# Layer 1 attention: VectorE does `finish` between the maxima and the row sums of a batch

## The chip, the core and the metric

The kernel runs on one core of a Trainium2 chip. The metric is the device time of one execution in microseconds (us). The engines are PE (TensorE, matrix products), DVE (VectorE), ACT (ScalarE), POOL (GpSimd) and SP (SyncE, which issues the DMAs here). Each engine runs its own list of instructions in order; engines wait for one another with semaphores that count up.

## What is computed

A four layer decoder with gated cross attention: x is 1024 x 128, the context 6404 x 128. Each layer adds an attention over the context and a feed forward block. The change lies in the attention of layer 1 alone:

```
mu = jnp.mean(x, axis=-1, keepdims=True)
var = jnp.mean(jnp.square(x - mu), axis=-1, keepdims=True)
xn = (x - mu) * jax.lax.rsqrt(var + EPS) * ln_g + ln_b
q = _split_heads(xn @ Wq)                    # 16 heads of 64
kv = xn @ Wkv
k = _split_heads(kv[..., :INNER])
v = _split_heads(kv[..., INNER:])
mem = _split_heads(memories @ Wm)
k = jnp.concatenate([k, mem], axis=2)        # 1024 + 6404 = 7428 keys
v = jnp.concatenate([v, mem], axis=2)
dots = jnp.einsum('bhid,bhjd->bhij', q, k) * scale
attn = jax.nn.softmax(dots, axis=-1)
out = jnp.einsum('bhij,bhjd->bhid', attn, v)
...
return out @ Wo + bo
```

## The kernel before

`l1_attention` works in 32 units. A unit is one head and one half (512) of the queries. The 7428 keys are 59 tiles of 128 (the last one of 4), and four tiles are a batch, so that a unit has 15 batches, 0 to 14.

In a batch PE does, in this order: two scorings for maxima (`max_score`, L893, bf16, each 128 queries against 1024 keys; they belong to a unit ahead), the exact scores of the four tiles (L915 and L916), an extra if the batch has one, and the weighing of the values of the batch before (L927). ACT turns each score tile into `prob` with Exp (L1031). The row sums of `prob` are shared out: DVE adds the first two tiles of a batch into `tot_d` (`total_up`, L1082; the unit's first tile is a copy, L1079), POOL the other two into `tot_p` (L1134). DVE also takes the maxima of the scorings out of PSUM (`maximum`, L1059), and the units' negated maximum (L1068) goes back through PE into the scores of the next unit.

An extra stands in a batch as `extra_of(u, b)` says. Batch 1 of every unit but the first has "fin": `finish(u - 1)`, in which PE multiplies the weighed values with Wo (L942) and sums the row sums over the partitions (L944), and DVE takes the reciprocal (L1092) and adds the result to y (L1095, four instructions). The other extras prepare the next pair of heads. With u mod 4 = 0 or 1, batches from 4 on (9 and 8 of them) have a "k": a K or Q projection on PE (L869), rounded by ACT (`round_hi`, L985), whose rest DVE takes (`cut_lo`, L1051). With u mod 4 = 3, batches 2 to 14 have a "v": a V projection (L882), copied out by ACT; with u mod 4 = 0 batches 0 and 2 have one too. The last four units have no "k", and no "v" from batch 2 on of unit 31.

Scorings for maxima and extras share two pairs of PSUM banks in turn. Whoever takes a pair waits for the one that had it two places earlier:

```
def take_slot(n):
    if n >= 2:
        by_dve, by_act = freed[n - 2]
        if by_act:
            pe.wait_ge(v_out, by_act)
        if by_dve:
            pe.wait_ge(released, by_dve)
    return slot(n)
```

So in a batch with an extra the order of the places is: first maximum scoring, second maximum scoring, extra. The extra waits for DVE's first maximum of its own batch, and the second maximum scoring of the next batch waits for the extra to be emptied: by `finish` (L1095) or `cut_lo` (L1051) on DVE, or by ACT. Within DVE's list, a batch is: two maxima, two row sums, the extra.

Of the kernel before, what the change touches and what calls it, by code (L numbers as in the profile page):

```python
# [588 lines left out]
def l1_attention(c, w, scratch):  # L589
# [32 lines left out]
    def f32(ap):  # L622
        return ap.bitcast(FP32)

    def rows_of(t):
        return min(P, KEYS - t * P)
# [4 lines left out]
    def extra_of(u, b):  # L631
        p, i = divmod(u, 4)
        if b == FIN_AT:
            return ("fin", u - 1) if u >= 1 else None
        if i == 0 and p >= 1 and b in (0, 2):
            return "v", (p, BATCHES - 2 + b // 2)
        if p + 1 == PAIRS:
            return None
        if i < 2 and 4 <= b <= 12 and 9 * i + b - 4 < JOBS:
            return "k", (p + 1) * JOBS + 9 * i + b - 4  # L640
        if i == 3 and b >= 2:
            return "v", (p + 1, b - 2)
        return None

    def max_steps(u, b):
        first = STEPS * (u + 1) + LEAD + PER_BATCH * b
        return [divmod(n, STEPS) for n in range(first, first + PER_BATCH) if n < STEPS * UNITS]
# [23 lines left out]
    def slot(n):  # L671
        return 4 + 2 * (n % 2)

    def ring_no(u, t):
        return 1 + (TILES + 1) * u + t + (1 if t >= BATCH * (NM_AT + 1) and u + 1 < UNITS else 0)

    def nm_no(u):
        return 0 if u == 0 else 1 + (TILES + 1) * (u - 1) + BATCH * (NM_AT + 1)

    def step_at(i):  # L680
        if i < UQ * FULL:
            return [(i // FULL, (i % FULL) * CH, CH)] * 2
        return [(2 * (i - UQ * FULL) + half, FULL * CH, REM) for half in range(2)]

    def dve_tiles(b):
        return [t for t in tiles_of(b) if t % BATCH < 2]
# [16 lines left out]
    with ExitStack() as held:  # L703
# [17 lines left out]
        with phase(nc, "loaded") as (block, loaded):  # L721
            @block.sync
            def _(sp):
                sp.dma_start(gain[:], w["ln_g"].partition_broadcast(P)).then_inc(loaded, 16)
                sp.dma_start(shift[:], w["ln_b"].partition_broadcast(P)).then_inc(loaded, 16)
                sp.dma_start(bo[:], w["bo"].partition_broadcast(P)).then_inc(loaded, 16)
                for base in (0, DH):
                    sp.dma_start(Wo_twice[0][base:base + DH, :], w["Wo"][0:DH, :]).then_inc(loaded, 16)
                sp.wait_ge(loaded, 16 * 9)
# [19 lines left out]
        with phase(nc, "chain", "scored", "exped", "weighed", "slotted", "released", "v_out", "hi_out", "cast_out",  # L749
# [104 lines left out]
            def _(pe):  # L854
# [9 lines left out]
                def project(k):  # L864
                    p, (kind, src, a, n, _) = k // JOBS, jobs[k % JOBS]
                    bank = take_slot(slot_no["k", k])
                    if p >= 1:
                        pe.wait_ge(weights_in[p % 2], 64 * ((p + 1) // 2))
                    nc.tensor.matmul(c.banks(bank)[:, 0:n], weights[p % 2][:, kind, :], src[:, a:a + n],  # L869
                                     start=True, stop=True).then_inc(slotted, 1)  # L870
# [173 lines left out]
            @block.vector  # L1044
            def _(dve):
                link = Chain(dve, chain)

                def cut_lo(k):
                    n, m = slot_no["k", k], jobs[k % JOBS][3]
                    dve.wait_ge(hi_out, k + 1)  # L1050
                    nc.vector.tensor_tensor(lo_s[k % DEPTH][:, 0:m], c.banks(slot(n))[:, 0:m],  # L1051
                                            f32(hi_s[k % DEPTH][:, 0:m]), ALU.subtract).then_inc(released, 1)

                def maximum(u, i):
                    n = slot_no["max", (u, i)]
                    dve.wait_ge(slotted, n + 1)
                    j, _, _ = step_at(i)[0]
                    if i < UQ * FULL:
                        nc.vector.tensor_reduce(mx[:, u % 2, j, i % FULL:i % FULL + 1], c.banks(slot(n), 2), AX.X,  # L1059
                                                ALU.max).then_inc(released, 1)  # L1060
                    else:
                        nc.vector.tensor_reduce(mx[:, u % 2, j:j + 2, FULL], c.ps[:, slot(n):slot(n) + 2, 0:REM], AX.X,
                                                ALU.max).then_inc(released, 1)
                    if i == STEPS - 1:
                        dve.wait_ge(released, freed[n][0])
                        if u >= 2:
                            dve.wait_ge(scored, nm_no(u - 2) + 1)
                        nc.vector.tensor_reduce(nm[:, u % 2, :], mx[:, u % 2, :, :], AX.X, ALU.max, negate=True  # L1068
                                                ).then_inc(nm_ready, 1)

                def total_up(u, b):
                    for t in dve_tiles(b):
                        r, count = rows_of(t), DVE_TILES * u + dve_tiles_before(t)
                        dve.wait_ge(exped, ring_no(u, t) + 1)
                        p = prob[0:r, (BATCHES * u + b) % 2, t % BATCH, :]
                        if t == 0:
                            if u >= 2:
                                dve.wait_ge(slotted, slot_no["fin", u - 2] + 1)
                            nc.vector.tensor_copy(tot_d[:, u % 2, :], p).then_inc(totalled_d, 1)  # L1079
                        else:  # L1080
                            dve.wait_ge(totalled_d, count)
                            nc.vector.tensor_tensor(tot_d[0:r, u % 2, :], tot_d[0:r, u % 2, :], p, ALU.add  # L1082
                                                    ).then_inc(totalled_d, 1)

                def dve_tiles_before(t):
                    return sum(x % BATCH < 2 for x in range(t))

                def finish(u):
                    n = slot_no["fin", u]
                    dve.wait_ge(slotted, n + 1)  # L1090
                    inv, f = rec[:, u % 2, :], u % HALVES
                    link(nc.vector.reciprocal(inv, c.banks(slot(n) + 1)[:, 0:UQ]))  # L1092
                    for j in range(UQ):
                        y = c.y[:, UQ * f + j, :]
                        last = nc.vector.scalar_tensor_tensor(out=y, in0=c.banks(slot(n))[:, j * P:(j + 1) * P],  # L1095
                                                              scalar=inv[:, j:j + 1], in1=y, op0=ALU.mult, op1=ALU.add)
                    last.then_inc(released, 1)

                nc.vector.memset(c.y[:], 0.0)
                for k in range(JOBS):  # L1100
                    cut_lo(k)
                for n in range(STEPS + LEAD):
                    maximum(*divmod(n, STEPS))
                for u in range(UNITS):
                    for b in range(BATCHES):
                        for step in max_steps(u, b):
                            maximum(*step)
                        total_up(u, b)
                        kind, what = extra_of(u, b) or (None, None)
                        if kind == "k":  # L1110
                            cut_lo(what)
                        if kind == "fin":
                            finish(what)
                finish(UNITS - 1)

            @block.gpsimd
# [34 lines left out]
        with phase(nc, "chain", "unused") as (block, chain, _):  # L1151
            @block.vector
            def _(dve):
                link = Chain(dve, chain)
                link(nc.vector.tensor_tensor(c.y[:], c.y[:], bo[:, None, :].to_broadcast([P, QT, D]), ALU.add))
                add_to_x(nc, link, c, c.y[:], c.gx[:, 1:2])
# [929 lines left out]
```

## Time and profile before

| | us |
|---|---|
| median of three runs (lowest, highest) | 5669.59 (5669.28, 5680.94) |
| the profiled execution, its time | 5678.92 |
| its span from first to last instruction | 5677.2 |
| PE busy in it | 5030.6 (89%) |
| DVE busy in it | 4761.7 (84%) |
| ACT busy in it | 3058.7 (54%) |
| POOL busy in it | 1553.8 (27%) |

Busy shares are averages over all layers. Layer 1's attention stands from about 440 to 2880 us of the span. What one of its waits is worth is read from the rows of that stretch.

### The profile page before, as it was taken

What the parts mean: (1) busy time and instruction counts of PE and PEld (TensorE: products, weight loads), DVE (VectorE), ACT (ScalarE), POOL (GpSimd) and SP (SyncE); (2) the same over time, 40 slices, a digit from 0 to 9 for tenths busy, and PEclk for the clock granted to TensorE, in tenths of its full rate; (3) what the DMA queues carried; (4) which work ended last, traced back from release to release, by engine and by line L of the source; (5) the groups of instructions that cost most, each with busy time, mean ns of one, the idle gap of its engine ahead of it and who ended that gap; (6) DMA issues with size and microseconds to landing.
All of it is one profiled execution on the core that took longest, in us unless ns stands there. A gap on an engine that the chain in (4) does not pass through costs nothing. (4 is left out here: it accounts for less than half of the span.)

```text
span 5677.2 us, 73839 instructions
## 1 busy us (share of the span) xinstructions
PE 5030.6 (89%) x26367; PEld 1906.1 (34%) x26376; DVE 4761.7 (84%) x4945; ACT 3058.7 (54%) x5929; POOL 1553.8 (27%) x1158
## 2 busy tenths in 40 slices
PE   8939999999999999999933699999996499999996
PEld 5524444545454544444411222222223122222222
DVE  7459989898989899898867899999972799999993
ACT  3314444444444444444410288888881078888883
POOL 0015656565656565565612000000000200000000
PEclk9969999999999999999965799999995599999996
DMA  0043233333324132322101311111100311111110
GB/s 30 1 130 101 67 91 88 92 89 83 107 61 129 45 117 57 100 76 53 35 4 35 74 24 23 28 24 27 24 9 7 98 25 24 28 24 24 24 19 6
DMA packets 176340, 298.47 MB, mean 53 GB/s; under 512 B 36732, under 2 KB 113992, under 8 KB 172904
## 3 DMA queue, kind: packets, MB, share of 16 engines
q1 hardware_dynamic: 171880, 292.44, 21.1%
q8 instruction: 214, 3.51, 0.3%
q10 hardware_dynamic: 4096, 1.29, 0.1%
q14 instruction: 150, 1.23, 0.1%
HBM read 178.92 MB, written 109.89 MB: 51 GB/s over the span
## 5 line engine op out<-in xcount | busy, mean ns | idle before, releaser
L1589 DVE TENSOR_REDUCE a_mx<-ps 128x1 f32<-128x1024 f32 x1536 | 1815.2, 1220 | 125.4 <-PE ps L1460 110.5
L1554 ACT ACTIVATE a_prob<-ps 128x512 f32<-128x512 f32 (+1 forms) x3264 | 1699.0, 602 | 388.0 <-PE ps L1448 383.3
L1031 ACT ACTIVATE prob<-ps 128x512 f32<-128x512 f32 (+1 forms) x1888 | 974.8, 603 | 1182.2 <-PE ps L916 1182.1
L1134 POOL TENSOR_TENSOR tot_p<-tot_p,prob 128x512 f32<-128x512 f32 (+1 forms) x896 | 1341.5, 1497 | 919.4 <-ACT prob L1031 854.4
L1059 DVE TENSOR_REDUCE mx<-ps 128x1 f32<-128x1024 f32 x896 | 1051.7, 1216 | 152.2 <-PE ps L893 144.8
L1082 DVE TENSOR_TENSOR tot_d<-tot_d,prob 128x512 f32<-128x512 f32 x928 | 1055.5, 1137 | 87.6 <-ACT prob L1031 36.1
L1460 PE MATMUL ps<-a_K,a_Q 51*128 51x512 bf16 (+1 forms) x3328 | 1086.1, 386 | 41.6 <-DMA a_Q<-q_stack_dram 29.7
L1448 PE MATMUL ps<-a_Q,a_K 51*128 51x512 bf16 (+1 forms) x3264 | 1004.9, 389 | 67.6 <-ACT a_prob L1554 61.6
L1484 PE MATMUL ps<-a_prob,a_V 128*9 128x512 f32 x6528 | 956.5, 610 | 10.6 <-ACT a_acc L1538 10.6
L927 PE MATMUL ps<-prob,V 128*64 128x512 f32 (+1 forms) x3776 | 934.0, 605 | 0.0
L915 PE MATMUL ps<-QA,KA 128*128 128x512 f32 (+1 forms) x1888 | 805.5, 427 | 0.0
L916 PE MATMUL ps<-QB,KB 128*128 128x512 f32 (+1 forms) x1888 | 749.1, 397 | 0.0
L1448 PEld LDWEIGHTS ps<-a_Q,a_K 51*128 51x128 bf16 (+1 forms) x3264 | 242.1, 94 | 1167.8 <-ACT a_prob L1554 966.1
L915 PEld LDWEIGHTS ps<-QA,KA 128*128 128x128 f32 (+1 forms) x1888 | 350.6, 186 | 303.8 <-issue 173.9
L927 PEld LDWEIGHTS ps<-prob,V 128*64 128x64 f32 (+1 forms) x3776 | 229.6, 136 | 465.7 <-issue 284.0
L893 PE MATMUL ps<-KM,QM 64*128 64x512 bf16 (+1 forms) x1920 | 311.7, 382 | 67.5 <-DVE y L1095 29.8
L916 PEld LDWEIGHTS ps<-QB,KB 128*128 128x128 f32 (+1 forms) x1888 | 353.9, 187 | 46.9 <-issue 0.3
L1460 PEld LDWEIGHTS ps<-a_K,a_Q 51*128 51x128 bf16 x3328 | 240.6, 94 | 319.6 <-DVE a_mx L1589 278.6
L1889 POOL MEMSET f_spread<- 8x512 f32 x1 | 0.5, 514 | 1230.8 <-DVE r_total L1852 1230.8
L1981 POOL MEMSET f_ones<- 128x128 f32 x1 | 0.2, 209 | 1221.6 <-DVE r_total L1852 1221.6
L893 PEld LDWEIGHTS ps<-KM,QM 64*128 64x128 bf16 x1920 | 73.4, 94 | 486.9 <-issue 482.2
L1484 PEld LDWEIGHTS ps<-a_prob,a_V 128*9 128x9 f32 x6528 | 106.3, 88 | 280.3 <-issue 239.7
(348 smaller groups left out, 3117.7 us busy)
## 6 DMA issues: line engine op xcount, KB each, us to landing
a_K<-k_stack_dram SPq DMA_DIRECT2D x64, 600.4 KB, 5.8
k_hi_dram<-hi_s SPq DMA_DIRECT2D x112, 256.0 KB, 2.0
k_lo_dram<-lo_s SPq DMA_DIRECT2D x112, 256.0 KB, 2.0
KA<-k_hi_dram SPq DMA_DIRECT2D x64, 384.0 KB, 4.3
KA<-k_lo_dram SPq DMA_DIRECT2D x64, 384.0 KB, 5.6
KB<-k_hi_dram SPq DMA_DIRECT2D x64, 384.0 KB, 6.5
k_bf_dram<-bf_s SPq DMA_DIRECT2D x112, 128.0 KB, 1.7
KM<-k_bf_dram SPq DMA_DIRECT2D x32, 448.0 KB, 7.1
```

Of the source, the lines that this page charges most:

```text
L915: nc.tensor.matmul(out, KA[:, cols], QA[u % 2][:], start=True, stop=False)
L916: nc.tensor.matmul(out, KB[:, cols], QB[u % 2][:], start=False, stop=True).then_inc(scored, 1)
L927: last = nc.tensor.matmul(c.banks(ACC)[DH * g:DH * (g + 1), :], V[0:r, t, DH * side:DH * (side + 1)], prob[0:r, (BATCHES * u + b) % 2, t % ...
L1031: nc.scalar.activation(prob[0:r, batch % 2, t % BATCH, :], c.banks(n % 3)[0:r, :], ACT.Exp, scale=SCALE).then_inc(exped, 1)
L1059: nc.vector.tensor_reduce(mx[:, u % 2, j, i % FULL:i % FULL + 1], c.banks(slot(n), 2), AX.X, ALU.max).then_inc(released, 1)
L1082: nc.vector.tensor_tensor(tot_d[0:r, u % 2, :], tot_d[0:r, u % 2, :], p, ALU.add).then_inc(totalled_d, 1)
L1134: nc.gpsimd.tensor_tensor(tot_p[0:r, u % 2, :], tot_p[0:r, u % 2, :], p, ALU.add).then_inc(totalled_p, 1)
L1448: nc.tensor.matmul(c.banks(n % 3)[0:r, :], K[(u // HALVES) % 2][0:ROWS, t * P:t * P + r], Q[u % 3][0:ROWS, :], start=True, stop=True).then ...
L1460: last = nc.tensor.matmul(c.banks(slot(step) + half)[:, 0:k], Q[u % 3][MROW:MROW + ROWS, j * P:(j + 1) * P], K[(u // HALVES) % 2][MROW:MRO ...
L1484: last = nc.tensor.matmul(c.banks(ACC)[32 * g:32 * g + VW, :], V[0:r, t, u // HALVES, :], prob[0:r, (BATCHES * u + b) % 2, g, :], start=(t ...
L1554: nc.scalar.activation(prob[0:r, batch % 2, t % BATCH, :], c.banks(n % 3)[0:r, :], ACT.Exp, scale=SCALE).then_inc(exped, 1)
L1589: nc.vector.tensor_reduce(mx[:, u % 2, j, i % FULL:i % FULL + 1], c.banks(slot(step), 2), AX.X, ALU.max).then_inc(maxed, 1)
```

## The change

In the loop of DVE over the batches, the extra of kind "fin" is done ahead of the row sums of its batch and no longer behind them. "k" stays behind. The slots and the counts in `freed` stay as they are, since `finish` still comes behind the maxima of its batch and ahead of those of the next.

```
                         for step in max_steps(u, b):
                             maximum(*step)
+                        kind, what = extra_of(u, b) or (None, None)
+                        if kind == "fin":
+                            finish(what)
                         total_up(u, b)
-                        kind, what = extra_of(u, b) or (None, None)
                         if kind == "k":
                             cut_lo(what)
-                        if kind == "fin":
-                            finish(what)
                 finish(UNITS - 1)
```

On DVE, in unit 1, from batch 1 on, the program before has these rows (L1059 are maxima, L1082 row sums, L1092 and L1095 are `finish`):

```order
L1059 TENSOR_REDUCE mx<-ps 128x1 x2
L1082 TENSOR_TENSOR tot_d<-tot_d,prob 128x512 x2
L1092 RECIPROCAL rec<-ps 128x4
L1095 SCALAR_TENSOR_TENSOR y<-ps,rec,y 128x128 x4
L1059 TENSOR_REDUCE mx<-ps 128x1 x2
L1082 TENSOR_TENSOR tot_d<-tot_d,prob 128x512 x2
```

The program with the change has at the same place:

```order
L1059 TENSOR_REDUCE mx<-ps 128x1 x2
L1092 RECIPROCAL rec<-ps 128x4
L1095 SCALAR_TENSOR_TENSOR y<-ps,rec,y 128x128 x4
L1082 TENSOR_TENSOR tot_d<-tot_d,prob 128x512 x2
L1059 TENSOR_REDUCE mx<-ps 128x1 x2
L1082 TENSOR_TENSOR tot_d<-tot_d,prob 128x512 x2
```

The five instructions of `finish` moved ahead of the two row sums, here and in 30 more units. On PE nothing moved; around the same place it has, before and after, the end of batch 1 (L942 and L944 are `finish`, L927 the weighing) and the start of batch 2:

```order
L942 MATMUL ps<-Wo_twice,acc 128x128
L944 MATMUL ps<-ones_col,tot_p 128x1
L927 MATMUL ps<-prob,V 64x512 x4
L893 MATMUL ps<-KM,QM 128x512 x4
L915 MATMUL ps<-QA,KA 128x512
```

The L893 of this piece are the two maximum scorings of batch 2, two matmuls each. The second of them takes the banks that `finish` used.

## Rows read from the trace of the kernel before

**Rows 1.** Busy time (and instructions) of each engine, 1000 to 2000 us; clock, DMA share, GB/s

```profile
1000.00:2000.00 1000.00, 986.09 (x4598) 478.85 (x4600) 902.64 (x902) 476.29 (x937) 592.92 (x439) 1.00 0.34 87
```

**Rows 2.** PE's waits over the span: who waits for whom, total us, times, longest

```profile
PE ps L893 <- DVE y L1095: 29.8, 23, 1.3
```

**Rows 3.** Timeline, PE, unit 10, batches 1 to 3: start, us, what, [idle before <-releaser]

```profile
1217.20 0.60 PE L893 MATMUL ps<-KM,QM 64*128 64x512 bf16 x4
...
1221.28 0.28 PE L944 MATMUL ps<-ones_col,tot_p 128*128 128x1 f32 x2
...
1223.36 0.39 PE L893 MATMUL ps<-KM,QM 64*128 64x512 bf16 x2
1225.05 0.39 PE L893 MATMUL ps<-KM,QM 64*128 64x512 bf16 x2 [1.29 <-DVE y L1095]
...
1229.33 0.61 PE L893 MATMUL ps<-KM,QM 64*128 64x512 bf16 x4
```

**Rows 4.** Timeline, DVE, the same place

```profile
1218.00 2.34 DVE L1059 TENSOR_REDUCE mx<-ps 128x1 f32<-128x1024 f32 x2
1220.26 3.39 DVE L1082 TENSOR_TENSOR tot_d<-tot_d,prob 128x512 f32<-128x512 f32 x2
1223.57 0.17 DVE L1092 RECIPROCAL rec<-ps 128x4 f32<-128x4 f32 x1
...
1224.82 2.35 DVE L1059 TENSOR_REDUCE mx<-ps 128x1 f32<-128x1024 f32 x2
```

**Rows 5.** Timeline, unit 10, batches without an extra: PE, then DVE, then POOL

```profile
1256.28 0.60 PE L893 MATMUL ps<-KM,QM 64*128 64x512 bf16 x4
...
1260.78 0.60 PE L893 MATMUL ps<-KM,QM 64*128 64x512 bf16 x4
...
1254.74 2.35 DVE L1082 TENSOR_TENSOR tot_d<-tot_d,prob 128x512 f32<-128x512 f32 x2
1257.02 2.34 DVE L1059 TENSOR_REDUCE mx<-ps 128x1 f32<-128x1024 f32 x2
1259.28 3.46 DVE L1082 TENSOR_TENSOR tot_d<-tot_d,prob 128x512 f32<-128x512 f32 x2
1262.67 2.34 DVE L1059 TENSOR_REDUCE mx<-ps 128x1 f32<-128x1024 f32 x2
...
1267.22 1.21 DVE L1059 TENSOR_REDUCE mx<-ps 128x1 f32<-128x1024 f32 x1
...
1254.74 3.50 POOL L1134 TENSOR_TENSOR tot_p<-tot_p,prob 128x512 f32<-128x512 f32 x2 [1.04 <-ACT prob L1031]
1259.24 2.96 POOL L1134 TENSOR_TENSOR tot_p<-tot_p,prob 128x512 f32<-128x512 f32 x2 [0.99 <-ACT prob L1031]
```

**Rows 6.** Timeline, POOL, unit 10, batches 0 and 1

```profile
1216.26 1.26 POOL L1134 TENSOR_TENSOR tot_p<-tot_p,prob 128x512 f32<-128x512 f32 x1
1220.15 2.95 POOL L1134 TENSOR_TENSOR tot_p<-tot_p,prob 128x512 f32<-128x512 f32 x2 [2.63 <-ACT prob L1031]
```

**Rows 7.** Line 1082 (DVE's row sums): duration in ns, least/median/most

```profile
L1082 DVE TENSOR_TENSOR tot_d<-tot_d,prob x928: 673/1103/1773, 443.2 to 2871.9; 128x512 f32<-128x512 f32 x186
```

**Rows 8.** Timeline, PE, unit 11, batch 3, with a V projection

```profile
1300.47 0.60 PE L893 MATMUL ps<-KM,QM 64*128 64x512 bf16 x4
...
1302.99 1.05 PE L882 MATMUL ps<-weights,ctxT 128*128 128x128 f32 x8
...
1305.84 0.39 PE L893 MATMUL ps<-KM,QM 64*128 64x512 bf16 x2
```

**Rows 9.** Timeline, unit 9, batches 4 and 5, with K projections: PE, then DVE

```profile
1155.80 0.61 PE L893 MATMUL ps<-KM,QM 64*128 64x512 bf16 x4
...
1158.33 1.02 PE L869 MATMUL ps<-ctxT,weights 128*128 128x512 f32 x2
...
1161.15 0.91 PE L893 MATMUL ps<-KM,QM 64*128 64x512 bf16 x4
...
1160.84 0.68 DVE L1051 TENSOR_TENSOR lo_s<-ps,hi_s 128x512 fp32r<-128x512 f32 x1
1161.58 2.36 DVE L1059 TENSOR_REDUCE mx<-ps 128x1 f32<-128x1024 f32 x2
```

## The prediction

> **What bounds the kernel now.** I read the busy time of the engines over one stretch first. From 1000 to 2000 us, inside layer 1's attention, PE is busy 98.6% of the time at full clock and DVE 90% [rows 1]. So PE sets the pace there, and only what PE waits for can be won. The list of PE's waits names one cause inside this phase that repeats: a maximum scoring (L893) waits for DVE's y (L1095), the last result of `finish`, 23 times with 29.8 us in total [rows 2]. The phase has 31 such places; 23 of them wait.
>
> Then I read one of them in order of time, in unit 10. I call c and d the two scorings for maxima of a batch and B the start of c. In batch 1 B is 1217.20; the last matmul of `finish` starts at 1221.28 and ends at 1221.56 [rows 3]. DVE does its maxima from 1218.00, then the two row sums for 3.39 us, and takes up `finish` only at 1223.57 [rows 4]. Batch 2 begins at 1223.36. Its d must reuse the banks of `finish` and starts at 1225.05. Undisturbed, d starts 0.22 behind c (four records of L893 take 0.61 us together, two take 0.39) [rows 3, 9], so the stall costs 1225.05 - 1223.58 = 1.47 us. The batch agrees: 5.97 us to 1229.33, where an undisturbed one takes 4.49 (1256.28 to 1260.78) [rows 5]. 23 x 1.47 = 34 us, 0.6% of the time, is the most that the change can bring.
>
> **The change, step by step, in unit 10.** No instruction is added or removed, no DMA moves, and PE, ACT, POOL and SP keep their order. On DVE `finish` passes the two row sums of batch 1, in 31 units.
>
> (a) New wait. DVE ends its maxima at 1218.00 + 2.34 = 1220.34 and now waits for PE's `finish`, 1221.56 plus 0.04 (a maximum starts 0.43 behind B, 1161.15 to 1161.58, and c's record takes 0.39) [rows 3, 9]. That is 1.26 us idle. Queued behind it are the two row sums and the maxima of batch 2. PE isn't held by it.
>
> (b) `finish` takes DVE 1.25 us (1223.57 to 1224.82), and PE resumes 1.48 us after its reciprocal. From 1221.60 that is 1223.08; PE wants d at 1223.58. The wait on y goes away with 0.50 us to spare.
>
> (c) Row sums. At their old place they met POOL's two sums, which ran from 1220.15 for 2.95 us [rows 6]. A row sum alone takes 0.68 us (the minimum), one that meets a POOL sum up to 1.77 [rows 7]. POOL's alone take 1.26 [rows 6], so without DVE's they end about 1220.15 + 1.27 + 0.14 + 1.27 = 1222.83. DVE starts its own at 1222.85: 0.68 + 0.10 + 0.68, and the next maximum starts 0.08 before the end, at 1224.23 against 1224.82 before. So the two contended sums get cheaper, which pays for the idle time and 0.6 us more.
>
> (d) But PE gains 1.47 us and DVE only 0.59. I call L the start of DVE's first maximum minus B: in a good batch 0.43 [rows 9], now 1224.23 - 1223.36 = 0.87. The first row sum starts at L + 2.26. POOL's first sum starts 2.96 after B (1256.28, 1259.24) [rows 5]. In the trace, DVE at 1254.74 starts with POOL and its pair takes 2.35; at 1259.28 it comes 0.04 behind POOL and the pair takes 3.46 [rows 5]. Whoever comes second waits for the other's whole instruction. Now DVE comes at 3.13, 0.17 behind POOL, in batch 2 of every unit. DVE's next maximum then starts 1262.67 - 1259.24 = 3.43 after POOL's start, so at B + 6.39, whatever L was.
>
> The Trainium skill (SBUF — State Buffer, SBUF: two separate sides) calls this an exclusive lock: a DVE instruction with two SBUF inputs and a GpSimd one that reads SBUF exclude each other for the whole instruction. The trace agrees, 3.46 against 2.35 us. If they only shared bandwidth, (d) would not hold and the gain would stay near the 34 us; this rule speaks against the change.
>
> (e) What L becomes by unit (kinds are u mod 4):
>
> - Kind 3 (units 3 to 27, seven, V projections): batches take 5.38 us, so L = 6.39 - 5.38 = 1.01 from batch 3 on. PE's projection 2.52 behind B (1300.47, 1302.99) [rows 8] needs c's maximum: L + 1.21 + 0.15 (what PE needs after a release: `cut_lo` ends at 1161.52, d starts at 1161.67 [rows 9]) = 2.37. Hidden by 0.15 us. Gain 7 x 1.47 = 10.3.
> - Kind 2 and units 29, 30 (nine, no projection behind batch 2): L = 6.39 - 4.49 = 1.90, as 1262.67 - 1260.78 = 1.89 shows. DVE's batch takes 4.55 (1262.67 to 1267.22), so L grows by 0.06. Near 2.1 the first row sum (L + 2.26) falls behind POOL's second sum (2.96 + 1.27 + 0.14 = 4.37), which puts L at about 2.41. PE's d needs L + 1.13 + 1.21 + 0.15 = L + 2.49 and wants 4.49 + 0.22 = 4.71; at 2.41 that is 4.90: stalls of about 0.18, every other batch, two or three a unit, 0.45. Gain 9 x 1.01 = 9.1.
> - Kind 1 (units 1 to 25, seven, K/Q projections from batch 4): L is 1.97 at batch 4. PE's projection wants its banks 2.53 behind B (1155.80, 1158.33) [rows 9] and gets them at 1.97 + 1.36 = 3.33: stall 0.80. DVE's first row sum starts at 4.24, behind POOL's first and ahead of its second; the pair takes 2.36 to 6.60, `cut_lo` (0.68 us) ends at 7.20, and the next d gets the banks at 7.35. The batch is now 5.35 + 0.80 = 6.15 long, so d stands at 1.20 instead of today's 0.52 (the 0.91 us of L893 at 1161.15 is 0.30 over 0.61): 0.68 more. Because d delays POOL as well, the row sums come first again and batch 6 is as before. Cost 1.48, gain 1.47: nothing.
> - Kind 0 (units 4 to 24, six, the same projections, but nothing to win: the 8 of the 31 places without a wait are the seven of this kind and unit 31): L is 1.01 or more at batch 3, enough to come behind POOL, and 1.90 at batch 4. The same costs, 0.73 + 0.68: 6 x 1.41 = 8.5 lost. Unit 28, without projections, loses about 0.3.
>
> Sum: -10.3 - 9.1 + 0.1 + 8.5 + 0.3 = -10.5 us. The profiled execution took 5678.9 us, 9.3 above the median of the three runs, so it would go to 5668.4; against the median 5669.6 that is 5659.1. I forecast 5659 us, 0.19% faster. About 0.2% (11.3 us) is what a measurement can tell from no change, so the forecast stands right at that edge.
>
> **Rivals.**
>
> No meeting in batch 2. If DVE's row sum came 0.18 us earlier, or POOL's sum as much later, (e) falls away: all stalls are won, 34 us, 5636 us. For it speaks that 0.17 us is the difference of two estimates (a) to (c), against it that each part has a row and that the sign held in both traced cases of (d). The Trainium skill (Perfetto Trace Analysis, GPSIMD Instruction) calls GpSimd's recorded spans unreliable; if the start at 2.96 is such a record, this rival gains. The traced starts tell apart who comes first to 0.04 us in (d), which speaks against a large error. Chance 0.17.
>
> Slower. In kind 3 the projection is covered by only 0.15 us. If each V batch lost one more turn to POOL (1.1 us, 3.46 against 2.35), L would be 2.1, the projection would stall 0.95 us in one batch and, since that stall gives DVE time, about half as much on average: 91 batches x 0.45 = 41 us, 5700 us. It decides from 0.24 us a batch on (22 us over my forecast). Against it: a stall of PE pushes POOL's sums back too, and DVE comes first again. Chance 0.06.
>
> The loss spreads. Kinds 2 and 3 give back most of what they win, as kind 1 does; then nothing is left against kind 0's 8.5 but some of the 19 us: about 5670 us, same. Chance 0.07.
>
> The stall stays. If PE still waited for y, nothing changes, 5670; it needs `finish` on DVE 0.5 us later than in (b). Chance 0.03.
>
> **How the numbers follow.** The walk of (e) has 0.67. Its own range is 5649 to 5668: the stall terms of kinds 0 and 1 (13 units x 1.4 us) are the largest with a sign against me; by half they move 9 us. It splits into 0.29 faster and 0.38 same. With the first rival's 0.17, faster is 0.46; with the last two, 0.07 and 0.03, same is 0.48; slower is 0.06. The range takes in the full gain below and no change above: 5634 to 5671.
>
> **What the profile would show.** Right: no wait of L893 for y; DVE's reciprocal (L1092) idle before it for PE's L944 in all 31 units, 1.0 to 1.6 us each, some 40 us; the first maximum of batch 2 at L near 0.87, POOL's sum there ahead of DVE's; then new waits of PE's L869 for the maximum of L1059, 13 times 0.4 to 0.8 us by the records, and of L893 for `cut_lo` of L1051, 13 times. Wrong: the first row sum of batch 2 taking 0.68 us (then 5636), or PE's L882 waiting for L1059 in kind 3 (then the slower one).

## The result

The kernel with the change takes 5666.4 us (median of 17 runs, 5645.0 to 5673.5), the kernel before 5673.2 (median of 17, 5667.9 to 5682.7). The ratio is 0.9981, its 95% interval 0.9972 to 0.9989: 0.19% faster, as forecast, and with an interval on both sides of the 0.2% that I had set as the edge. The ratio is estimated from all runs; the quotient of the two medians alone is 0.9988 (6.7 us), which is inside the interval too.

In 1000 to 2000 us of the profile after, PE is busy 99.0% (98.6% in [rows 1]) and DVE 92.5%, POOL 56.9% against 59.3% (columns as in [rows 1]):

```profile
1000.00:2000.00 1000.00, 990.35 (x4616) 480.28 (x4614) 925.08 (x906) 477.75 (x940) 568.93 (x439) 1.00 0.34 87
```

The wait of [rows 2] is gone from PE's list. These two waits stand in it and weren't there before, or hardly (total us, times, longest):

```profile
PE ps L893 <- DVE lo_s L1051: 10.2, 14, 0.8
...
PE ps L869 <- issue: 7.2, 13, 0.6
```

The wait on `cut_lo` was 0.2 us, once, before; 13 of its 14 places now, and all 13 at the projection, are in the 13 units of kinds 0 and 1 that have projections, in batches 5 and 4. The second is listed as "issue" and not as a wait for DVE's maximum: the list of waits alone doesn't name its cause.

The sharpest measure is the phase itself, from the first to the last weight load of L942, which stands once in every `finish`. The row of that line (least, median and longest in ns, then first and last start) in the kernel before:

```profile
L942 PEld LDWEIGHTS ps<-Wo_twice,acc x256: 186/192/192, 522.6 to 2877.4; 128*128 128x128 f32 x128
```

and in the kernel after:

```profile
L942 PEld LDWEIGHTS ps<-Wo_twice,acc x256: 186/192/192, 525.5 to 2869.5; 128*128 128x128 f32 x128
```

The phase went from 2354.8 to 2344.0 us, by 10.8; I had forecast 10.5. The spans, 5677.2 and 5663.0, differ by 14.2 us; the other 3.4 lie in stretches that the change doesn't touch (2.9 us more ahead of the first L942, 6.3 less behind the last).

Unit 10 after the change, batches 1 to 3, first on PE:

```profile
1217.86 0.60 PE L893 MATMUL ps<-KM,QM 64*128 64x512 bf16 x4
...
1224.02 0.61 PE L893 MATMUL ps<-KM,QM 64*128 64x512 bf16 x4
1228.53 0.60 PE L893 MATMUL ps<-KM,QM 64*128 64x512 bf16 x4
```

then on DVE (in brackets the idle time before and what ended it):

```profile
1218.66 2.34 DVE L1059 TENSOR_REDUCE mx<-ps 128x1 f32<-128x1024 f32 x2
1222.26 0.18 DVE L1092 RECIPROCAL rec<-ps 128x4 f32<-128x4 f32 x1 [1.26 <-PE ps L944]
1222.48 1.13 DVE L1095 SCALAR_TENSOR_TENSOR y<-ps,rec,y 128x128 f32<-128x128 f32 x4
1223.52 1.48 DVE L1082 TENSOR_TENSOR tot_d<-tot_d,prob 128x512 f32<-128x512 f32 x2
1224.91 2.35 DVE L1059 TENSOR_REDUCE mx<-ps 128x1 f32<-128x1024 f32 x2
1227.18 3.31 DVE L1082 TENSOR_TENSOR tot_d<-tot_d,prob 128x512 f32<-128x512 f32 x2
```

and on POOL:

```profile
1220.81 2.69 POOL L1134 TENSOR_TENSOR tot_p<-tot_p,prob 128x512 f32<-128x512 f32 x2 [2.63 <-ACT prob L1031]
1226.98 2.96 POOL L1134 TENSOR_TENSOR tot_p<-tot_p,prob 128x512 f32<-128x512 f32 x2 [3.48 <-ACT prob L1031]
```

Steps (a) to (d) of the prediction can be read here. DVE idles 1.26 us ahead of the reciprocal. PE's batch 2 is 4.51 us long and was 5.97 [rows 3]. The row sums of batch 1 take 1.48 us instead of 3.39. The first maximum of batch 2 is 1224.91 - 1224.02 = 0.89 late, and the first row sum starts at 1227.18, 0.20 behind POOL's 1226.98, so that the pair takes 3.31 us.

### The profile page after: what moved, and what is told of

The parts are those of the page before. It is cut to its first block and busy times, and to the rows that moved or that the text cites. A ratio compares the mean times of both kernels' runs of the same rounds, so it can differ in the third digit from the quotient of the medians.

```text
span 5663.0 us, 73839 instructions
## 1 busy us (share of the span) xinstructions
PE 5030.4 (89%) x26367; PEld 1908.2 (34%) x26376; DVE 4787.5 (85%) x4945; ACT 3058.9 (54%) x5929; POOL 1490.5 (26%) x1158
## 5 line engine op out<-in xcount | busy, mean ns | idle before, releaser
L1134 POOL TENSOR_TENSOR tot_p<-tot_p,prob 128x512 f32<-128x512 f32 (+1 forms) x896 | 1272.1, 1420 | 972.4 <-ACT prob L1031 907.4
L1082 DVE TENSOR_TENSOR tot_d<-tot_d,prob 128x512 f32<-128x512 f32 x928 | 1088.9, 1173 | 83.7 <-ACT prob L1031 31.9
L1059 DVE TENSOR_REDUCE mx<-ps 128x1 f32<-128x1024 f32 x896 | 1050.6, 1214 | 82.1 <-PE ps L893 77.1
L1484 PE MATMUL ps<-a_prob,a_V 128*9 128x512 f32 x6528 | 953.6, 608 | 10.8 <-ACT a_acc L1538 10.7
L927 PE MATMUL ps<-prob,V 128*64 128x512 f32 (+1 forms) x3776 | 934.0, 605 | 0.0
L927 PEld LDWEIGHTS ps<-prob,V 128*64 128x64 f32 (+1 forms) x3776 | 229.6, 136 | 465.3 <-issue 293.8
L893 PE MATMUL ps<-KM,QM 64*128 64x512 bf16 (+1 forms) x1920 | 311.9, 383 | 46.6 <-DVE mx L1059 17.0
L893 PEld LDWEIGHTS ps<-KM,QM 64*128 64x128 bf16 x1920 | 76.7, 94 | 465.9 <-issue 459.1
```

Of the source, the lines that this page charges most:

```text
L927: last = nc.tensor.matmul(c.banks(ACC)[DH * g:DH * (g + 1), :], V[0:r, t, DH * side:DH * (side + 1)], prob[0:r, (BATCHES * u + b) % 2, t % ...
L1134: nc.gpsimd.tensor_tensor(tot_p[0:r, u % 2, :], tot_p[0:r, u % 2, :], p, ALU.add).then_inc(totalled_p, 1)
L1484: last = nc.tensor.matmul(c.banks(ACC)[32 * g:32 * g + VW, :], V[0:r, t, u // HALVES, :], prob[0:r, (BATCHES * u + b) % 2, g, :], start=(t ...
```

## The experiments

In all of them I read the phase, from the first to the last L942 (2354.8 us before, 2344.0 with the change), beside the measured ratio to the kernel before. The ratio has an interval of 0.2 to 0.3% because the whole time wanders from run to run (5645.0 to 5673.5 us with the change, 0.5%); the phase is one profiled execution of each.

### The change by kinds of unit

```
                         kind, what = extra_of(u, b) or (None, None)
+                        early = u % 4 in (2, 3) or u == 29
-                        if kind == "fin":
+                        if kind == "fin" and early:
                             finish(what)
                         total_up(u, b)
                         if kind == "k":
                             cut_lo(what)
+                        if kind == "fin" and not early:
+                            finish(what)
```

> The change only in units with u mod 4 of 2 or 3 and in unit 29; the others keep the old order. Theory (what is won depends on what stands behind batch 2 of the unit): 7 units win 1.47 us, 9 win 0.97, nothing is lost elsewhere, so 19 us under the kernel before, ratio 0.9966, and 8 to 9 us under the change in all units. Rival (DVE is what bounds the phase, so a PE stall that is removed comes back later wherever it stood): about half of the full change, -5 us, ratio 0.9991.

The other half has `early = u % 4 in (0, 1) and u != 29`.

> The change only in units with u mod 4 of 0 or 1, without unit 29. Theory: 7 units of kind 1 end at 0.0 each (won 1.47, lost 1.47), 6 of kind 0 lose 1.31 each, unit 28 loses 0.4: 8 us slower than before, ratio 1.0015. PE's waits for y stay 16 times and the late projections (L869 at 3.2 to 3.3 us behind the start of their batch) stand 13 times. Rival (the same gain for each removed wait on y): 7 x 1.47 = 10 us faster, 0.9982.

Kinds 2 and 3 alone: ratio 0.9979 (0.9970 to 0.9988).

```profile
L942 PEld LDWEIGHTS ps<-Wo_twice,acc x256: 186/192/192, 522.0 to 2859.6; 128*128 128x128 f32 x128
```

The phase is 2337.6 us, 17.2 shorter than before; expected were 19, the rival's 5 is out. The measured ratio, forecast 0.9966, is less good than its phase (17.2 of 5670 us would be 0.9970), at the edge of the interval.

Kinds 0 and 1 alone: ratio 1.0022 (1.0013 to 1.0032).

```profile
L942 PEld LDWEIGHTS ps<-Wo_twice,acc x256: 186/192/192, 521.7 to 2885.5; 128*128 128x128 f32 x128
```

2363.8 us, 9.0 longer than before; expected were 8. Seven stalls on y were taken away there, and the kernel is slower. The two halves add up to -8.2 us, near the -10.8 of the whole change. 2.3 us of the difference are in batch 1 of six units in each half (3, 7, 11, 15, 29, 30 and 3, 7, 11, 19, 23, 30), which takes 6.36 us (unit 11: 1281.68 to 1288.04) instead of 6.17. The difference begins in batch 0: DVE's copy (L1079) and POOL's row sum start within 0.03 us of each other, and either may win. DVE, then POOL, in unit 11 with the change and with kinds 2 and 3 alone:

```profile
1286.21 0.42 DVE L1079 COPY tot_d<-prob 128x512 f32<-128x512 f32 x1
1286.20 1.55 POOL L1134 TENSOR_TENSOR tot_p<-tot_p,prob 128x512 f32<-128x512 f32 x1
...
1280.77 1.52 DVE L1079 COPY tot_d<-prob 128x512 f32<-128x512 f32 x1
1280.75 1.26 POOL L1137 TENSOR_TENSOR tot_p<-tot_p,prob 128x512 f32<-128x512 f32 x1
```

Where DVE's copy takes 1.52 us, DVE's first maximum of batch 1 is 1.32 behind the batch instead of 1.09, and the batch is 6.36 long; this holds for every such unit of all ten profiles. There are none in the kernels before and after, five with POOL's wait, eight with `finish` between the row sums, one with `cut_lo` there too, none with the addition left out, three with the large filler, five with the small one: up to 1.5 us of a phase are chance of this kind. So the sign of the change depends on what stands behind batch 2: a projection in batch 4 loses it.

### POOL waits in batch 2

```
                 def total_up(u, b):
+                    if b == 2 and u >= 1:
+                        pool.wait_ge(totalled_d, dve_totals(u, b))
                     for t in pool_tiles(b):
```

> The change in all units, and in batch 2 of each unit but the first POOL waits for DVE's two row sums before it begins its own. One wait is added on POOL, nothing is taken away. Theory (the loss comes from DVE's row sum finding POOL's one running in batch 2): DVE's pair takes 1.5 us there instead of 3.3, the first maximum of batch 3 starts 0.43 behind the start of the batch, and all stalls are won: -34 us, ratio 0.9940. Rival (DVE is late because of the idle time that the change puts ahead of its reciprocal): batch 3 stays late, ratio 0.998 as with the change alone, or more since POOL is later now.

Ratio 0.9957 (0.9944 to 0.9969), phase 2323.0 us: 31.8 shorter than before, 21.0 shorter than the change alone.

```profile
L942 PEld LDWEIGHTS ps<-Wo_twice,acc x256: 186/192/192, 521.6 to 2844.6; 128*128 128x128 f32 x128
```

DVE in unit 9, from `finish` on:

```profile
1134.37 0.18 DVE L1092 RECIPROCAL rec<-ps 128x4 f32<-128x4 f32 x1 [1.26 <-PE ps L944]
...
1135.63 1.48 DVE L1082 TENSOR_TENSOR tot_d<-tot_d,prob 128x512 f32<-128x512 f32 x2
1137.03 2.35 DVE L1059 TENSOR_REDUCE mx<-ps 128x1 f32<-128x1024 f32 x2
1139.29 1.47 DVE L1082 TENSOR_TENSOR tot_d<-tot_d,prob 128x512 f32<-128x512 f32 x2
1141.05 2.36 DVE L1059 TENSOR_REDUCE mx<-ps 128x1 f32<-128x1024 f32 x2 [0.28 <-PE ps L893]
```

The idle time ahead of the reciprocal is still there, 1.26 us. The row sums of batch 2 take 1.47 instead of 3.31, and at batch 3 DVE waits for PE again. One wait more, on an engine that has slack, and nearly all 34 us are there. So the rival falls: the loss of 21 us came from the meeting with POOL in batch 2, not from the idle time.

### POOL starts later in batch 2, by a filler

POOL fills a tile that nobody reads, between its wait for `prob` and its first row sum of batch 2.

```
                         pool.wait_ge(exped, ring_no(u, t) + 1)
+                        if b == 2 and t % BATCH == 2 and u >= 1:
+                            nc.gpsimd.memset(filler[:], 0.0)
                         p = prob[0:r, (BATCHES * u + b) % 2, t % BATCH, :]
```

> The change in all units, and POOL fills a tile of its own that nobody reads (128x256, memset) in batch 2 of each unit, between its wait for prob and its first row sum: work added, nothing taken away, no wait added. The page has memsets of 128x128 in 0.21 us and 128x1 in 0.10 us, so POOL's sum starts some 0.3 us later, at about 3.3 behind the start of batch 2, and DVE's comes at 3.15. Theory (who starts first decides): DVE's first row sum takes 0.68 us there, the late projections of kinds 0 and 1 go away, and the phase from the first to the last L942 is about 2323 us, 21 under the change and 32 under the kernel before. Rival (POOL's work and the span of its sums count, not their order): 2344 us or more, as with the change.

> As e7_pool_filler_256 with a tile of 128x1: some 0.1 us. POOL's sum starts at 3.05 to 3.1 and is still ahead of DVE's at 3.15, if only by a few hundredths. Theory: nothing is won, the phase stays at 2344 us, late projections stay 13 times. If the delay is more than 0.2 us it falls on the other side and gives 2323. Nothing between the two is expected. Rival (the loss grows smoothly with the overlap of the two sums): about 2337.

The small filler (128x1): ratio 0.9995 (0.9986 to 1.0004), phase 2347.4 us by the row of that line, L943 here. In unit 9:

```profile
1148.45 3.35 DVE L1083 TENSOR_TENSOR tot_d<-tot_d,prob 128x512 f32<-128x512 f32 x2
...
1148.23 0.10 POOL L1129 MEMSET filler<- 128x1 f32 x1 [3.46 <-ACT prob L1032]
1148.29 2.96 POOL L1137 TENSOR_TENSOR tot_p<-tot_p,prob 128x512 f32<-128x512 f32 x2
```

It delays POOL by only 0.06 us. POOL is ahead by 0.16 instead of 0.20, and nothing is won; the rival's 2337 is out. The phase is even 3.4 us longer than with the change, of which five batches of 6.36 us are 1.0.

The large filler (128x256): ratio 0.9973 (0.9962 to 0.9983), phase 2336.4 us:

```profile
L943 PEld LDWEIGHTS ps<-Wo_twice,acc x256: 186/192/337, 522.7 to 2859.1; 128*128 128x128 f32 x128
```

Here neither theory met the number. POOL's added work makes the phase 7.6 us shorter than with the change alone (the ratios, 0.9973 and 0.9981, have intervals that overlap) and 11.0 us shorter than with the small filler, where the medians differ by 11.5 (5645.1 and 5656.7 us), but 2323 was expected. Unit 9, batches 2 and 3, DVE and then POOL:

```profile
1144.04 2.36 DVE L1083 TENSOR_TENSOR tot_d<-tot_d,prob 128x512 f32<-128x512 f32 x2
1146.33 2.34 DVE L1060 TENSOR_REDUCE mx<-ps 128x1 f32<-128x1024 f32 x2
1148.59 3.24 DVE L1083 TENSOR_TENSOR tot_d<-tot_d,prob 128x512 f32<-128x512 f32 x2
...
1143.81 0.31 POOL L1129 MEMSET filler<- 128x256 f32 x1 [3.45 <-ACT prob L1032]
1144.08 3.47 POOL L1137 TENSOR_TENSOR tot_p<-tot_p,prob 128x512 f32<-128x512 f32 x2
1148.32 2.96 POOL L1137 TENSOR_TENSOR tot_p<-tot_p,prob 128x512 f32<-128x512 f32 x2 [0.77 <-ACT prob L1032]
```

In batch 2 DVE starts 0.04 ahead of POOL and its pair takes 2.36, as the theory has it. But DVE doesn't catch up: from maximum to maximum it needs 1146.33 - 1141.77 = 4.56 us and PE's batch is 4.49, so in batch 3, without a filler, it comes 0.27 behind POOL. The meeting is put off by a batch. Only where batch 2 has a V projection (5.26 or 5.38 us long) is there time to catch up. The waits of L893 on `cut_lo` fall from 14 to 8 and those of the projection listed as "issue" from 13 to 7: kind 0 is mended, kind 1 is not. Then 7 x 1.47 (kind 3) + 9 x 0.97 (kind 2 and units 29 and 30) = 19 us are left, and 18.4 were measured, with three batches of 6.36 us (0.6) in it.

### One addition of `finish` left out

This kernel doesn't compute a quarter of y; it is read for its time alone.

```
-                    for j in range(UQ):
+                    for j in range(UQ - 1):
                         y = c.y[:, UQ * f + j, :]
```

> The change in all units, and finish on DVE leaves out the last of its four additions to y (a quarter of y is not computed, so this is a probe of time alone). DVE is free 0.26 us earlier in batch 1, and nothing else is touched. Theory (what decides is whether DVE's first row sum of batch 2 starts before or behind POOL's, 0.17 to 0.2 us apart under the change): it now starts at 2.88 us behind the start of the batch, ahead of POOL's 2.96, takes 0.68 us, and all stalls are won: the phase from the first to the last L942 is about 32 us shorter than before the change (with the change it is 10.8 shorter), ratio 0.994 to 0.996. Rival (DVE's load counts in proportion): 31 x 0.26 = 8 us more than the change, 19 us under the kernel before, ratio 0.9967.

Ratio 0.9983 (0.9974 to 0.9992), phase 2868.5 - 524.1 = 2344.4 us: neither. 8 us of DVE's work were taken away and the phase didn't move. DVE and POOL in unit 9:

```profile
1143.10 0.87 DVE L1095 SCALAR_TENSOR_TENSOR y<-ps,rec,y 128x128 f32<-128x128 f32 x3
1143.89 1.58 DVE L1082 TENSOR_TENSOR tot_d<-tot_d,prob 128x512 f32<-128x512 f32 x2
1145.39 2.35 DVE L1059 TENSOR_REDUCE mx<-ps 128x1 f32<-128x1024 f32 x2
1147.65 3.47 DVE L1082 TENSOR_TENSOR tot_d<-tot_d,prob 128x512 f32<-128x512 f32 x2
...
1141.44 2.68 POOL L1134 TENSOR_TENSOR tot_p<-tot_p,prob 128x512 f32<-128x512 f32 x2 [2.63 <-ACT prob L1031]
1147.61 2.97 POOL L1134 TENSOR_TENSOR tot_p<-tot_p,prob 128x512 f32<-128x512 f32 x2 [3.48 <-ACT prob L1031]
```

What I had missed: starting 0.26 us earlier, at 1143.89, DVE's row sum now runs into the end of POOL's pair of batch 1 (1141.44 + 2.68 = 1144.12), and its own pair takes 1.58 instead of 1.48. In batch 2 it is then 0.04 us behind POOL instead of 0.20, and that is as good as 0.20: the pair takes 3.47. The rival, which counts DVE's load, falls. The theory's rule stands, but my number for the start was off: DVE starts 3.00 behind the batch and not 2.88, mostly by that 0.10 us, and it was enough.

### `finish` between the two row sums

```
-                def total_up(u, b):
-                    for t in dve_tiles(b):
+                def total_up(u, b, part=slice(None)):
+                    for t in dve_tiles(b)[part]:
...
+                        total_up(u, b, slice(0, 1))
                         if kind == "fin":
                             finish(what)
-                        total_up(u, b)
+                        total_up(u, b, slice(1, 2))
```

> DVE takes its work of a batch in the order maxima, first row sum, finish, second row sum, in all units; POOL as before the change. Theory: the first row sum fills the time in which DVE would wait for PE's finish (in kinds 1, 2 and 3 it meets POOL and ends 4.8 us behind the start of batch 1, so finish releases PE at about 6.3 where 6.38 is wanted), and batch 2 begins with the first maximum 0.45 to 0.5 late, ahead of POOL's sum: all 23 stalls of 1.47 are won and none comes back, -34 us, ratio 0.9940. Rival: finish comes too late by a few tenths (a small wait on y of 0.1 to 0.3 us stays) and DVE meets POOL in batch 2 after all: -10 us, 0.998.

Ratio 0.9954 (0.9940 to 0.9967), phase 2844.8 - 521.7 = 2323.1 us, 31.7 shorter than before. In unit 10 DVE has no idle time left ahead of the reciprocal (in kind 0, where the first row sum comes early, 1.0 us is left, unit 12):

```profile
1207.45 2.34 DVE L1059 TENSOR_REDUCE mx<-ps 128x1 f32<-128x1024 f32 x2
1209.72 1.71 DVE L1082 TENSOR_TENSOR tot_d<-tot_d,prob 128x512 f32<-128x512 f32 x1
1211.35 0.17 DVE L1092 RECIPROCAL rec<-ps 128x4 f32<-128x4 f32 x1
1211.56 1.13 DVE L1095 SCALAR_TENSOR_TENSOR y<-ps,rec,y 128x128 f32<-128x128 f32 x4
1212.60 0.68 DVE L1082 TENSOR_TENSOR tot_d<-tot_d,prob 128x512 f32<-128x512 f32 x1
1213.26 2.36 DVE L1059 TENSOR_REDUCE mx<-ps 128x1 f32<-128x1024 f32 x2
1215.53 2.36 DVE L1082 TENSOR_TENSOR tot_d<-tot_d,prob 128x512 f32<-128x512 f32 x2
```

The first row sum still meets POOL (1.71 us), but in time that would be idle. Batch 2 starts on PE at 1212.82, its first maximum 0.44 behind, and the row sum at 1215.53 is ahead of POOL's at 1215.78. The mechanism is as expected; the ratio forecast was 0.9940, at the end of the interval, the phase 2 us short of the forecast, of which the eight batches of 6.36 us are 1.5.

### `cut_lo` between them too

The same, with `cut_lo(what)` also ahead of `total_up(u, b, slice(1, 2))`.

> As e4_between, and cut_lo too stands between the two row sums of its batch. Theory: PE's second maximum scoring no longer waits for the banks of the projection (0.29 and 0.23 us in every second batch with a projection, four to five times in each of 13 units behind the first finish): the phase from the first to the last L942 becomes 14 us shorter than with e4_between (2323.1), ratio to the kernel before 0.993 by the measured 0.9954 less 0.25%. What could undo it: cut_lo waits until ACT has rounded the projection, 4.17 us behind the start of the batch, so the second row sum comes behind POOL's second and the next batch starts 1.05 late; its projection needs 1.16 or less. Rival: that margin fails and PE waits at L869 for the first maximum, no gain over e4_between, 0.9954.

Ratio 0.9917 (0.9904 to 0.9929), 5617.8 us against 5665.4: the fastest kernel of this study.

```profile
L942 PEld LDWEIGHTS ps<-Wo_twice,acc x256: 186/192/337, 524.5 to 2831.3; 128*128 128x128 f32 x128
```

The phase is 2306.8 us, 16.3 less than with `finish` alone between; 14 were expected. Seven fewer batches of 6.36 us are 1.3 of it. No wait of L893 on `cut_lo` is left, and batches with a projection are all 5.34 to 5.37 us long. PE in unit 9:

```profile
1148.40 0.61 PE L893 MATMUL ps<-KM,QM 64*128 64x512 bf16 x4
1150.93 1.03 PE L869 MATMUL ps<-ctxT,weights 128*128 128x512 f32 x2
1153.76 0.60 PE L893 MATMUL ps<-KM,QM 64*128 64x512 bf16 x4
```

DVE's maximum starts at 1149.55 there, 1.15 behind the batch, later than my 1.05 and still within the 1.16 that the projection allows. 1.15 is the latest in any batch with a projection; the margin is thin.

## Why the prediction was right

The path of the prediction came out term by term, as below. That the ratio agrees with the forecast to 0.01% is luck, since its interval is 0.0017 wide; the phase, 10.8 us against 10.5, is the better support. That the kernel is faster is clear of the interval; whether by more or less than the 0.2% of the edge was open in the forecast (0.46 and 0.48) and stays open.

**The stall and its size.** 23 stalls of 1.47 us were counted as 34 us. With the late row sums out of the way, 31.8 and 31.7 us came (POOL waiting, `finish` between). That is the bound, within 2.3 us, of which five and eight batches of 6.36 us are 1.0 and 1.5.

**(a) and (b), the new wait.** DVE idles 1.26 us in unit 10 and PE isn't held: its wait on y is gone in all 23 places. Over the phase the reciprocal waits 47.8 us in 32 places, of which 5.3 at the last; I had said some 40 in 31.

**(c) The row sums get cheaper.** 1.48 us against my 1.46, the maximum 0.89 behind the batch against my 0.87.

**(d) The meeting in batch 2.** DVE 0.20 behind POOL, forecast 0.17. That this, and not the idle time, costs the 21 us is shown by POOL's wait (2344.0 to 2323.0 us), and that order decides and not load by the left out addition, which gave nothing for 8 us of work.

**(e) By kinds.** From batch 2 of a unit to batch 2 of the next (of unit 30 to the last L942), the kernel after against the kernel before: kind 3 won 10.2 us in its seven units (forecast 10.3); kind 2 with units 29 and 30 won 8.8 (9.1), having lost again 0.5 us a unit in batches 9, 11 and 12; kind 1 came out even (forecast: 0.1 lost); kind 0 lost 7.9 (8.5) and unit 28 0.4 (0.3). Together that is 10.7. The errors of the terms are 0.6 us at most. In the experiments kinds 2 and 3 with unit 29 won 17.2 us alone (forecast 19.4), kinds 0 and 1 lost 9.0 (8.9). In the kernel after, unit 9 has a projection in batch 4 at 3.27 behind its start (I had 3.33), on DVE's maximum at 1.95 (1.97), and in batch 5 the second maximum scoring at 1.17 (1.20). PE there:

```profile
1155.00 0.60 PE L893 MATMUL ps<-KM,QM 64*128 64x512 bf16 x4
1158.27 1.10 PE L869 MATMUL ps<-ctxT,weights 128*128 128x512 f32 x2 [0.57 <-issue]
1161.16 0.39 PE L893 MATMUL ps<-KM,QM 64*128 64x512 bf16 x2
1162.33 0.39 PE L893 MATMUL ps<-KM,QM 64*128 64x512 bf16 x2 [0.77 <-DVE lo_s L1051]
...
1167.45 0.61 PE L893 MATMUL ps<-KM,QM 64*128 64x512 bf16 x4
```

Batches 4 and 5 are 12.45 us, and were 10.99 from 1155.80 to 1166.79 before: 1.46 lost, as much as batch 2 won. In kind 3 the maximum is 0.99 behind the batch (1299.68 against PE's 1298.69, forecast 1.01), and no projection is late, so the slower rival didn't come.

**What was wrong.** The first rival's price. I gave 34 us for the case that DVE came first in batch 2. The large filler made the second form of that case (POOL later), and it gave 18.4, since DVE has no time in a plain batch to catch up and comes second in batch 3. The price would have been 5651 us and not 5636, which makes the low end of the range too low. It had a chance of 0.17, and the forecast doesn't rest on it. I had also named the waits at L869 as waits for L1059; the list calls them "issue". That they come from the late maximum is seen by their going away with it: none is left in the profiles in which DVE is on time at batch 4 (POOL's wait, `finish` between), and seven, those of kind 1, with the large filler.

**What stays open.** The total of each run holds stretches that the change doesn't touch and that differ between executions by up to 21 us (3322.4 us outside the phase in the profile before, 3301.6 in that of kinds 2 and 3 alone); why the gains by the ratios (0.9957 and 0.9954) come out smaller than the 31.8 us of the phase, which would be 0.9944, was not tried. The record shows only where it happens: in the six experiments measured on one chip (both halves, POOL's wait, `finish` between, both fillers) the ratio is 0.0006 to 0.0013 above what the phase gives, in the two on another chip (`cut_lo` between too, the addition left out) 0.0001 and 0.0002. The phase of the kernel before is taken from one profile, and not once for each chip.

## What to carry to other kernels

A wait that is removed from the engine that sets the pace is won only if the engine behind it gains as much time as well. Here DVE gained 0.6 us where PE gained 1.5, so DVE came later, lost a turn to POOL, and gave it back at the next place where PE needs DVE early: read how late the second engine is at each such place, not only whether it waits. Between two engines that exclude each other, as these row sums do, the start order matters and not the load: 0.04 us behind costs as much as 0.20, 0.02 us may fall either way, and a longer step put into idle time (the first row sum ahead of `finish`) is better than a shorter one behind it.

## What was unexpected of the hardware

Work added to POOL made the phase 7.6 us shorter than with the change alone (2344.0 to 2336.4 us), and 8 us of DVE's work taken away made it no shorter (2344.4).

A row sum of DVE that starts 0.03 us or more behind a POOL row sum, and over 0.2 us before its end, ends 0.54 to 0.56 us after POOL's record ends, whenever it started: so it was in all 4984 such cases of the ten profiles. With 0.68 us for a row sum alone, one that starts 0.23 us before POOL's end is therefore lengthened by only 0.10 us (0.78), and in the kernel after those that start up to 0.11 us before it are not lengthened (0.67 to 0.69). The 36 that started within 0.02 us behind POOL's start were not held at all; POOL's was. The copy of batch 0 at 0.02 us was held in one execution and not in another.

A memset of 128x1 on POOL has a record of 0.10 us, yet the next instruction starts 0.06 us after the memset's start.
